# The setup, the edge loop and the last expert of a graph-network kernel, rearranged on one core

## What the reference computes

```python
xn = layernorm(x)
# edge weights, softmax-shifted, summed into a dense matrix; counts likewise
W[dst, src] += exp(edge_weight - max); CNT[dst, src] += 1
q, k, v = elu(xn @ Wq + bq) + 1, elu(xn @ Wk + bk) + 1, xn @ Wv + bv
attn = q @ (k.T @ v) / (q @ k.sum(0) + eps)          # 8 heads of 64
h = xn + attn @ Wo + bo; h = norm(h); h = h + ffn(h)  # a dense block
for l in range(3):                                    # three SAGE layers
    h = norm(mean_over_edges(relu(h @ Wp + bp)) @ Wl + bl + h @ Wr)
y = h + sum(gate_top2[e] * ffn_e(norm(h)) for e in range(8))
# then a sigmoid attention, a gated message step over W, and two banks
# of eight experts with one expert for each node
```

## Time and profile before

| | us |
|---|---|
| runs: median of 3 (lowest, highest) | 1845.51 (1834.01, 1851.74) |
| the profiled execution: its time | 1841.88 |
| its span in the trace | 1840.2 |
| mean granted TensorE clock | 0.949 of full speed |
| busy: PE, DVE, ACT, POOL | 1604.1, 1001.3, 420.1, 328.4 |

### The profile page before, as it was taken

How to read it: one execution, slowest core, us unless ns; L and a number is a source line. 1 busy time by engine, 2 the same in 40 slices (tenths; PEclk the granted TensorE clock), 3 DMA queues, 4 the chain that set the end, 5 groups by cost and what they waited for, 6 DMA issues and landing times.

```text
span 1840.2 us, 23095 instructions
## 1 busy us (share of the span) xinstructions
PE 1604.1 (87%) x8839; PEld 1225.3 (67%) x8839; DVE 1001.3 (54%) x1749; ACT 420.1 (23%) x798; POOL 328.4 (18%) x198
## 2 busy tenths in 40 slices
PE   1798877786989799979987999977999998599998
PEld 0677767666757677867765788866767656365665
DVE  6777677777963762384264666773245314641222
ACT  2422111222311220120113332333225001311121
POOL 2101012052210111012010122120211100003554
PEclk9899999997989899989997999988999999789999
DMA  3213223441230010001020010110101230555332
GB/s 109 96 37 108 84 96 118 138 131 36 81 129 0 24 40 24 1 23 42 11 80 24 23 46 24 47 46 1 46 24 71 89 117 20 204 187 164 48 66 36
DMA packets 51266, 123.72 MB, mean 67 GB/s; under 512 B 8003, under 2 KB 28378, under 8 KB 44151
## 3 DMA queue, kind: packets, MB, share of 16 engines
q1 hardware_dynamic: 14735, 66.64, 10.2%
q10 hardware_dynamic: 26570, 45.35, 7.0%
q0 software_dynamic: 9856, 10.28, 3.3%
HBM read 92.71 MB, written 40.22 MB: 72 GB/s over the span
## 4 chain that ended last, share of the span: by engine, by line
PE 73%; DVE 13%; DMA 7%; issue 3%; ACT 2%; DVEq 1%; PEld 0%; SPq 0%; POOL 0%; PEldq 0%; POOLq 0%; ACTq 0%
PE ps L598 8%; PE ps L599 8%; PE ps L600 8%; DMA arena<-d_kv 4%; PE ps L656 4%; PE ps L2143 4%; PE ps L658 4%; PE ps L609 4%; PE ps L2846 4%; PE ps L610 3%; PE ps L611 3%; PE ps L898 3%; PE ps L2820 3%; PE ps L787 2%; DMA arena<-d_w 1%
## 5 line engine op out<-in xcount | busy, mean ns | idle before, releaser
L2702 POOL CAST wslot<-arena 128x2048 fp32r<-128x2048 f32 x29 | 57.8, 1995 | 1093.7 <-PEq L2788 1072.0
L598 PE MATMUL ps<-wslot,XH 128*125 128x512 f32 (+2 forms) x560 | 216.1, 386 | 8.6 <-DVE XL L1364 7.0
L599 PE MATMUL ps<-wslot,XH 128*125 128x512 f32 (+2 forms) x560 | 213.4, 381 | 0.0
L600 PE MATMUL ps<-wslot,XL 128*125 128x512 f32 (+2 forms) x560 | 213.0, 380 | 0.0
L609 PE MATMUL ps<-XH,wslot 128*128 128x500 f32 (+1 forms) x336 | 124.0, 369 | 33.7 <-DVE XL L1364 31.9
L2704 POOL TENSOR_TENSOR wslot<-arena,wslot 128x2048 fp32r<-128x2048 f32 x29 | 135.0, 4655 | 2.3
L2143 PE MATMUL ps<-arena 125*128 x1330 | 96.5, 228 | 40.5 <-DVE arena L2398 31.5
L598 PEld LDWEIGHTS ps<-wslot,XH 128*125 128x125 f32 x560 | 105.4, 188 | 35.8 <-DVE XL L1364 8.7
L656 PE MATMUL ps<-CTr,Hhi 125*128 125x500 f32 (+1 forms) x360 | 125.0, 361 | 0.0
L610 PE MATMUL ps<-XH,wslot 128*128 128x500 f32 (+1 forms) x336 | 123.0, 366 | 0.0
L611 PE MATMUL ps<-XL,wslot 128*128 128x500 f32 (+1 forms) x336 | 121.8, 363 | 0.0
(11 more groups left out here) (427 smaller groups left out, 3096.2 us busy)
## 6 DMA issues: line engine op xcount, KB each, us to landing
arena<-in_units SPq DMA_DIRECT2D x29, 1024.0 KB, 4.8
arena<-in_units SPq DMA_DIRECT2D x8, 2048.0 KB, 12.2
d_w<-arena ACTq DMA_DIRECT2D x10, 625.0 KB
d_wt<-arena ACTq DMA_DIRECT2D x10, 625.0 KB, 4.0
rows<-in_rows ACTq DMA_DIRECT2D x22, 256.0 KB, 3.9
d_kv<-V SPq DMA_DIRECT2D x20, 250.0 KB
arena<-d_kv SPq DMA_DIRECT2D x20, 250.0 KB
arena<-d_wt ACTq DMA_DIRECT2D x2, 2441.4 KB
```

The costliest lines, as they stand in the source:

```text
L598: pe.matmul(o, lhsT=xh[:, k, s], rhs=H4[:, k, 0:nw], start=k == 0, stop=False, skip_group_check=True)
L599: pe.matmul(o, lhsT=xh[:, k, s], rhs=L4[:, k, 0:nw], start=False, stop=False, skip_group_check=True)
L600: last = pe.matmul(o, lhsT=xl[:, k, s], rhs=H4[:, k, 0:nw], start=False, stop=k == K - 1, skip_group_check=True)
```

## The change

- **Queries.** `DENSE` interleaves differently, and only eight of the twelve query products stand ahead of the loop (`AHEAD`). Products 8 to 11 follow the visits of blocks 0 to 3, in bank 7. Keys move to blocks 5 to 14, values to 16 to 25, K^T V to 28 to 37, the key sum to 38.
- **Limits.** Both engines load the limits of ten blocks at once (20 registers): once in the setup, and inside blocks 9, 19 and 29, on TensorE between the visits and the drain, on DVE behind the one-hots.
- **Setup by groups.** x comes in three loads on SP (tiles 0 to 3 ahead of unit 0, the rest behind it); statistics, root, scale, normalization and store go group by group, and the three `weighted_part` steps are cut in halves with query outputs in between. ACT's small loads come earlier.
- **Units 0 to 3** are split by ACT (high) and DVE (low) in place of POOL: unit 0 in the setup, 1 in blocks 3 and 4, 2 in blocks 14 and 15, 3 in blocks 25 and 27.
- **Group sums** come one block later and ahead of that block's read; the last group's after the attention rows.
- **Readback.** K and V tiles come back with two pairs in flight. The base is reloaded at block 38.
- **First expert.** DVE finishes the gate ahead of the bias add (L1622), and `wb` stands behind u3, not u5.
- **Last expert.** u0 to u3, d0 to d3, u4, u5, d4 to d7, the turns of tiles 0 to 3, d8, d9, then the query product.

The core of the diff:

```diff
-DENSE = ([("turn", t) for t in range(4)] + [("q", i) for i in range(2)] + [("turn", t) for t in range(4, 8)]
-         + [("q", i) for i in range(2, 5)] + [("turn", t) for t in range(8, NT)] + [("q", i) for i in range(5, 12)]
+DENSE = ([("turn", t) for t in range(4)] + [("q", i) for i in range(3)] + [("turn", t) for t in range(4, 8)]
+         + [("q", i) for i in range(3, 6)] + [("turn", t) for t in range(8, NT)] + [("q", i) for i in range(6, 12)]
...
+IN_LOOP = {i - AHEAD: ("q", i) for i in range(AHEAD, 12)}
+IN_LOOP.update({5 + t: ("k", t) for t in range(NT)})
+IN_LOOP.update({16 + t: ("v", t) for t in range(NT)})
+IN_LOOP.update({28 + t: ("kv", t) for t in range(NT)})
+IN_LOOP[38] = ("ks", 0)
...
         def load_bounds(eng, regs, g):
-            eng.reg_load(regs, bnd_i[0:1, 8 * g:8 * g + 8])
+            eng.reg_load(regs, bnd_i[0:1, 2 * PER * g:2 * PER * g + 2 * PER])
...
 # TensorE, block b
+                if b % PER == PER - 1 and b + 1 < NB:
+                    bounds = load_bounds(pe, regs, (b + 1) // PER)
                 pe.drain().then_inc(blk_full, 1)
                 if b in IN_LOOP:
...
+                    elif kind == "q":
+                        dense_cols(t, *weights)
...
 # DVE, setup
+            for i in range(3):
+                if i < 2:
+                    if i == 0:
+                        dve.wait_ge(bounds_ready, 4)
+                        bounds = load_bounds(dve, regs, 0)
+                        for t in GROUPS[0]:
+                            turn_low(t)
+                    x_stats(i + 1)
+                    x_spread(i + 1)
...
+                    next_part(i)
+                    x_scale(i + 1)
...
+                weigh(i, 0)
+                q_out(3 * i)
+                weigh(i, 1)
                 settle()
+                if i < 2:
+                    q_out(3 * i + 1)
+                    q_out(3 * i + 2)
+                    for t in GROUPS[i + 1]:
+                        turn_low(t)
+            dve.sem_inc(pre_ready, 1)
...
 # DVE, iteration b, behind the one-hots
+                if b % PER == PER - 1 and b + 1 < NB:
+                    bounds = load_bounds(dve, regs, (b + 1) // PER)
+                if b in (4, 15, 27):
+                    unit_low({4: 1, 15: 2, 27: 3}[b])
                 if b - 1 in IN_LOOP:
                     kind, t = IN_LOOP[b - 1]
+                    if kind == "q":
+                        q_out(t)
...
+                if b >= 5 and b % 4 == 1:
+                    dve.wait_ge(w_reduced, b - 1)
+                    group_sums((b - 5) // 4)
                 if b >= 1:
                     read_block(b - 1)
...
 # ACT, iteration b, behind the copy of the counts
+                if b - 1 in IN_LOOP and IN_LOOP[b - 1][0] == "q":
+                    query_exp(IN_LOOP[b - 1][1])
...
+                if b in (3, 14, 25):
+                    split_high({3: 1, 14: 2, 25: 3}[b])
-                if b == 37:
+                if b == 38:
...
 # SP, readback
-                        if t:
-                            sp.wait_ge(kv_loaded, 32 * t)
-                        sp.dma_start(K0t[:, t, :], d_kv[:, 0, t, :]).then_inc(kv_loaded, 16)
-                        sp.dma_start(R2t[:, t, :], d_kv[:, 1, t, :]).then_inc(kv_loaded, 16)
+                        if t >= 2:
+                            sp.wait_ge(kv_loaded[t % 2], 32 * (t // 2))
+                        sp.dma_start(K0t[:, t, :], d_kv[:, 0, t, :]).then_inc(kv_loaded[t % 2], 16)
+                        sp.dma_start(R2t[:, t, :], d_kv[:, 1, t, :]).then_inc(kv_loaded[t % 2], 16)
...
 # TensorE, experts of the first mixture
+                up_jobs(e, w, range(4))
                 if e == 0:
                     pe.wait_ge(top_ready, 1)
                     for i in range(6):
+                        weight_job(i)
+                if e == E0 - 1:
+                    down_jobs(e, w, GROUPS[0])
+                up_jobs(e, w, range(4, 6))
+                if e < E0 - 1:
+                    down_jobs(e, w, range(NT))
+                else:
+                    down_jobs(e, w, GROUPS[1])
+                    turn_group("t6", 5, 0, lambda t: R1t[:, t, :])
+                    down_jobs(e, w, GROUPS[2])
```

More of the change, by code:

```diff
@@ L431, in program @@
         rows_loaded = sem("rows_loaded")
-        x_in = [sem(f"x_in{i}") for i in range(2)]
+        x_in = [sem(f"x_in{i}") for i in range(3)]
         x_var = sem("x_var")
@@ L446, in program @@
         staged_out = [sem(f"staged_out{i}") for i in range(2)]
-        kv_loaded = sem("kv_loaded")
+        kv_loaded = [sem(f"kv_loaded{i}") for i in range(2)]
         ktot_added = sem("ktot_added")
@@ L1653, in gelu_low, with up @@
                         .then_inc(hidden_low, 1)
-                for i in range(6):
+                def up(i):
                     c0, w = CH[i // 2]
@@ L2087, in graph_pe @@
             pe.wait_ge(bounds_ready, 4)
-            for name in DENSE[4:NT + 12]:
+            regs = [pe.alloc_register(f"pe_bound{i}") for i in range(2 * PER)]
+            bounds = load_bounds(pe, regs, 0)
+            for name in DENSE[4:NT + AHEAD]:
                 if name[0] == "turn":
@@ L2093, in graph_pe @@
                     dense_cols(name[1], *weights)
-            unit_done()
             pe.wait_ge(pre_ready, 1)
             mores = pe.alloc_register("pe_mores")
-            regs = [pe.alloc_register(f"pe_bound{i}") for i in range(8)]
             pe.reg_mov(mores, 0)
@@ new lines, in x_spread, with x_scale @@
+            def x_spread(g):
+                t0, t1 = GROUPS[g][0], GROUPS[g][-1] + 1
+                settle()
+                for t in GROUPS[g]:
+                    own(dve.bn_aggr(mv[0:TP, 2 * t:2 * t + 2], bnst[0:TP, 6 * t:6 * t + 6]))
+                settle()
+                dve.sem_inc(x_var, 1)
+                own(dve.tensor_scalar(u10[0:TP, t0:t1], var[:, t0:t1], LN_EPS, None, ALU.add))
+            def x_scale(g):
+                t0, t1 = GROUPS[g][0], GROUPS[g][-1] + 1
+                r, u, v = rstd[0:TP, t0:t1], u10[0:TP, t0:t1], t10[0:TP, t0:t1]
+                dve.wait_ge(x_std, g + 1)
+                own(dve.reciprocal(r, std[0:TP, t0:t1]))
+                settle()
+                own(dve.tensor_tensor(v, r, r, ALU.mult))
+                settle()
+                own(dve.scalar_tensor_tensor(v, u, -0.5, v, ALU.mult, ALU.mult))
+                settle()
+                own(dve.scalar_tensor_tensor(r, v, 1.5, r, ALU.add, ALU.mult))
+                settle()
+                own(dve.scalar_tensor_tensor(nbias[0:TP, t0:t1], mu[:, t0:t1], -1.0, r, ALU.mult, ALU.mult))
+                settle()
+                dve.sem_inc(x_scaled, 1)
@@ L2308, in graph_dve @@
+            x_stats(0)
             dve.wait_ge(turn_full, 2)
             dve.tensor_reduce(bnd_c[0:2 * NB, 0:1], ps[0:2 * NB, 2, 0:NCH], X_AXIS, ALU.max).then_inc(bounds_ready, 1)
[L2310 to L2316 removed]
@@ L2341, in weighted_part @@
[L2341 to L2351 removed]
+            x_spread(0)
@@ L2372, in graph_dve, with turn_low @@
-            regs = [dve.alloc_register(f"dve_bound{i}") for i in range(8)]
-            dve.reg_mov(mores, 0)
+            x_scale(0)
+            bounds_to_registers()
+            unit_low(0)
+            own(dve.tensor_tensor(pre[:, 0:NCH, 0, :], iota_d[0:TP, :].unsqueeze(1).to_broadcast([TP, NCH, BW]),
+                                  dlow.unsqueeze(2).to_broadcast([TP, NCH, BW]), ALU.is_equal))
+            def turn_low(t):
+                s = slice(TP * t, TP * t + TP)
+                dve.wait_ge(x_high, t + 1)
+                dve.tensor_tensor(X0L[:, :, s], ps[:, DENSE_BANK[DJ[("turn", t)]], 0:TP * KC]
+                                  .rearrange("p (k e) -> p k e", k=KC), X0H[:, :, s].bitcast(F32), ALU.subtract)\
+                    .then_inc(dn_free, 1)
@@ new lines, in next_part, with weigh @@
+            def next_part(i):
+                own(dve.tensor_copy(hbf[i], exw))
+                settle()
+                if i < 2:
+                    own(dve.tensor_tensor(exw, exw, hbf[i], ALU.subtract))
+            def weigh(i, half):
+                c = slice(85 * half, 85 * half + 85)
+                own(dve.tensor_tensor(pre[:, c, 1 + i, :], pre[:, c, 0, :],
+                                      hbf[i][:, c].unsqueeze(2).to_broadcast([TP, 85, BW]), ALU.mult))
+            mores = dve.alloc_register("dve_mores")
@@ new lines, in graph_dve, with one_hot, group_sums @@
+            dve.sem_inc(pre_ready, 1)
+            dve.reg_mov(mores, 0)
+            def one_hot(buffer, c, b):
+                return dve.tensor_scalar(buffer, iota_s[0:TP, :], srcx[:, bass.ds(c, 1)], -float(BLK * b),
+                                         ALU.subtract, ALU.is_equal)
+            for i in range(VIS):
+                one_hot(oh[i], bounds[0][0] + i, 0).then_inc(oh_ready, 1)
+            q_out(AHEAD - 1)
+            def group_sums(g):
+                own(dve.tensor_reduce(rs[:, g, :], wst[g % 2], X_AXIS, ALU.add))
```

(1 more changed line is left out.)

333 lines of the change are left out of this document (157 added, 176 removed).

## The result

The changed kernel takes 1834.37 us in the median, the kernel before, timed beside it, 1841.95: a ratio of 0.9957, interval 0.9941 to 0.9974. That is 8 us faster where 22 were forecast.

What follows compares the result with a forecast made beforehand. TensorE was taken as the bound (73% of the chain of waits), VectorE in the setup. Setup -15.5, loop +7, after it -1.5, first expert -3, last -9 sum to -22: 1822 us forecast, range 1798 to 1845.

Steps and rivals of the forecast that it cites:

- Setup: Setup up to block 0: first query product at about 32, block 0 full at about 77.5, 15.5 us earlier.
- The rival of a setup at 85: Setup gains only half, with VectorE and ACT waiting on each other: block 0 full at 85, total 1829; chance 0.13.
- Query blocks: Edge loop, blocks 0 to 5: 6.6 us per block through ACT's passes, VectorE's output and read; 32.8 in all.
- Loads: Loads of limits in blocks 9, 19 and 29: by-register cost 5.8 us, each priced at 7 with slower clock behind.
- The flat price: Rival: a limit load costs the same whatever it holds, three stalls of 1 instead of 7 us; 1803, chance 0.25.
- the credit set against them: Key and value blocks: old loads and group sums held TensorE for 5.4 us of 143.8, leaving 138.4.
- fourteen blocks of about 4.75: Readback phase, blocks 25 to 39: TensorE's own work bounds again; 84.5 us including a load of 7.
- After the loop: Behind block 39: last group sums leave the attention rows' path, base reloaded a block later; -1.5 us, between -2.9 and +2.
- Experts: First expert -3 us from hidden work moved forward; last expert -9 from its query product's wait of 8.86.
- two pairs gain nothing: Rival: readback pair period stays at 7.8 us, readback ends 16 to 17 later; 1838, chance 0.12.
- The clock rival: Rival: TensorE falls to 1.2 GHz through the loop; ten half-clock blocks are +26 us, total 1848; chance 0.10.
- loop +13.4: Edge loop as a whole: block 39 full 269.7 us after block 0 against 262.6, so a loss of 7.

Runs made afterwards that it cites:

- e11: Changed kernel with limits of four blocks loaded at once, at the start of a round on both engines: 1830.3 us, 0.9918 of the kernel before.
- e5: Changed kernel with limits of four blocks at once (8 registers) instead of ten, still ahead of the drain: 1851.8 us, 1.0056 of the kernel before.
- e9: Changed kernel with the loop's group sums reducing only 8 of 128 columns, the rest left out: 1825.6 us, 0.9921 of the kernel before.
- e1: Changed kernel with the group sums behind the read of the block's weights, not ahead of it: 1836.1 us, 0.9983 of the kernel before.
- e6: Changed kernel with ScalarE's three loads of rows issued behind the attention rows, not ahead of them: 1835.0 us, 0.9967 of the kernel before.
- e10: Changed kernel with both expert edits (first and last expert) undone: 1845.4 us, 1.0020 of the kernel before.
- e7: Changed kernel with one pair of the readback in flight, as before the change: 1854.3 us, 1.0051 of the kernel before.
- e16: Changed kernel with limits of four blocks at once; TensorE loads at the start of a round, VectorE ahead of its read: 1838.3 us, 0.9980 of before.
- e2: Changed kernel with the ten-block limit loads at the end of the round, behind TensorE's drain and VectorE's read: 1834.4 us, 0.9959 of the kernel before.
- e3: Changed kernel with query products 8 to 11 alternating between two banks and put out one round later: 1825.2 us, 0.9922 of the kernel before.
- e12: Changed kernel with VectorE's low parts of units 1 to 3 behind that round's read: 1836.3 us, 0.9966 of the kernel before.
- e13: Changed kernel with query products in two banks, put out one round later, and row loads behind the attention: 1824.2 us, 0.9896 of the kernel before.
- e4: Changed kernel with all twelve query products ahead of the loop: 1829.4 us, 0.9929 of the kernel before.
- e14: Changed kernel with four-block limits at round start, two query banks with output one round later, row loads behind the attention: 1819.5 us, 0.9893 of before.
- e17: Changed kernel with limits of four blocks at once; VectorE loads at the start of a round, TensorE ahead of the drain: 1848.2 us, 1.0024 of before.

## Why the prediction was wrong

*Setup (-15.5, was -17.6)*: right in its steps; most of the 2.1 is block 0's visits and VectorE's earlier end. One reading was wrong: the row has PEclk 1.00, not the half clock that I read from it; no term of the sum hangs on it. Which of the setup's edits gave how much no run separates. The rival of a setup at 85 fell. In the rows above a switch of ScalarE's table is over in 1.29 us, 39.69 to 40.98, and no 1380 ns of drain stand behind it. The Trainium skill ("ScalarE: Activation LUTs", What ACT_TABLE_LOAD costs) has about 2.66 for a switch; the measurement decides, so the sum rightly went by the row.

*Query blocks (32.8, were 35.6)*: the step of 6.6 was right, its cause only half. I had VectorE's read in the ring; the next query product's one bank closes it as well, with 1.89 of wait in each round, and the two ways end within half a us of each other. So the agreement at 6.6 is in part luck. What the section didn't weigh is what the edit was worth by itself: moved back ahead of the loop, the four products give 9 to 10 us.

*Loads (three of 7, size right)*: against e11 the steps to blocks 9 and 10, 19 and 20, 29 and 30 are 7.6, 5.3 and 6.8 longer, 19.7 in all. The flat price fell: 1942 ns for 8 registers (e5) and 4992 for 20 are 254 for each further register. The Trainium skill ("Runtime: NRT & Kernel Launch", Instruction fetch mechanics) has about 200, for loads from HBM; the 254 here, for loads from SBUF, lie a quarter above it. What failed is the credit set against them, "The old loads and the group sums ... held TensorE for an estimated 5.4". Blocks 5 to 25 took 155.7; less the 12.9 of their two loads 142.8 are left, not 138.4, so the credit came to 1.0 (143.8 before). e11 says the same from the other side: with 19.7 for three loads and 15.5 to 17.7 for the edit as a whole, the nine cost about 2 to 4 at their old place. It is the largest single loss in the change; the sum held the cost of the loads and took back too much.

*The step that failed most*: "Then TensorE's own work bounds again: fourteen blocks of about 4.75". Blocks 25 to 39 took 91.6 instead of 84.5. In every fourth round VectorE has one-hots, 3.0 of group sums and the read, and TensorE waits for it, 0.71, 2.00 and 2.00 us ahead of blocks 30, 34 and 38. I had counted the sums only where they leave the path after the loop, not in the rounds that the faster readback had made short. e9 shows it: with the sums thin the waits ahead of 30 and 34 are gone and the stretch takes 86.1. e1 shows that their order isn't the matter, though it was my first theory. The rest is the clock, and it isn't the same in every profile: here the visits of blocks 34 and 38 ran partly at half clock (4.5 for 2.96), in e6 and e10 those of block 34 did not after the same 2.00 of wait, and the stretch took 89.7 and 89.6. No run sets the clock apart.

*After the loop (-1.5, was +3.7)*: the sums' place on the path was taken by ScalarE's three issues, 3.27 us. I had named the reload of the base, but not what stands on ScalarE's queue. e6 gives 3.7 back up to the last division, but not up to the gate, where the same code varies by 4.7 from profile to profile. So neither the +3.7 nor the gain of 1.5 is shown there.

*Experts (-12)*: nearly right, 11 in the time (e10), 8.8 in this trace. Of the first expert's 3 the trace shows 1.2, and other profiles with the same code 2.8 to 4.4.

*Rivals*: that two pairs gain nothing fell (e7: 10.5 to 12.6 at block 39). The clock rival in its full form fell, but a part of it stands: the granted clock from 80 to 360 is 0.94 before and 0.92 after, by my estimate at most 280 x 0.02 = 5.6 us. The rows of this stretch, kernel before, then changed with a row that the last section uses (us, engines, PEclk, DMA share, GB/s):

```profile
80.00:360.00 280.00, 223.36 (x2565) 197.33 (x2564) 202.82 (x308) 44.31 (x91) 32.34 (x16) 0.94 0.28 95
```

```profile
80.00:360.00 280.00, 224.20 (x2488) 197.75 (x2489) 197.06 (x300) 51.16 (x97) 12.60 (x10) 0.92 0.27 89
1640.00:1650.00 10.00, 10.00 (x32) 4.84 (x30) 2.07 (x3) 0.00 (x0) 0.00 (x0) 1.00 0.39 131
```

Of the terms of the sum that makes loop +13.4, after the loop +5.2, experts +3.2, setup -2.1 beyond the forecast, together 19.7; with the rest's -0.6, from -22 to -3.0 in this trace. The medians stand 7.6 apart, and the median before was 1841.95 with more runs than the 1845.51 that I had added 3.6 for.

## What to carry to other kernels

A stall that a trace shows beside other work has a price only at its place: before joining nine short loads into three long ones, read what covers each, and keep a load off the queue ahead of the mark that others wait for (e16: 12 us for nine loads). When a transfer is taken off the path, list every engine's work of the rounds that get shorter, not TensorE's alone; here VectorE's sums held TensorE for up to 2.0 us a group, and without them a store on ScalarE's queue came next. A step moved into a loop brings its buffer and its place in every queue with it: four products in one bank made a ring of three engines, which two banks and an output one round later opened.

## What the runs showed of the hardware

The 80 us from 1600 to 1680 hold a difference that no edit explains. This is the row 1640 to 1650 of the run e2:

```profile
1640.00:1650.00 10.00, 10.00 (x18) 4.84 (x17) 1.38 (x2) 0.00 (x0) 0.00 (x0) 0.50 0.11 31
```

In both kernels TensorE is busy 10.00 of 10 us from 1640 to 1650, yet the changed kernel had PEclk 1.00 and did 32 matmuls, e2 0.50 (1.2 of 2.4 GHz) and 18. From the second attention's keys to the end the runs take either 551.5 to 555.1 us (before, changed, e3, e6, e9, e10, e12, e13) or 560.5 to 565.8 (e1, e2, e4, e5, e7, e11, e14 to e17), and the granted clock from 1600 to 1680 is 0.91 to 0.96 in the first and 0.79 to 0.87 in the second. So up to 14 us of a single execution are this stretch, and a gain in the loop shows in the time only beside it: e11 had its block 39 15.5 us earlier and its time 4 lower. What sets the clock there remains open. It may be part of why e5, with block 39 full as late as in the changed kernel, lies 17 us above it; that it has this stretch more often was not tried.

A load of twenty registers on VectorE took 5083 ns in the setup, 4481 in block 19, 4559 in block 29, and 9998 in block 9; in every run with ten limits the steps to blocks 9 and 10 were 21.5 to 22.3 us together. A store of 625 KB was moving over ScalarE's queue in block 9. It isn't DMA traffic as such: during the load in block 29 the readback moved 124 GB/s, more than the 90 in block 9. Whether stores are the cause was not tried. Short loads have the same spread: ten loads of 8 registers on VectorE took 1841 to 3442 ns in e16.
